# Sliding attention: where the score mask is added, and who copies the unrotated half of the queries

## The chip, the cores and the metric

One core of one Trainium2 chip runs the whole program. The metric is the device time of an execution in microseconds (us); of several executions the median counts.

## The reference, cut to what matters

The program applies eight layers to x (four batches of 512 tokens, 512 features): four attentions and four feed-forward blocks. The change lies in the last attention, which looks back over a window of 128 tokens, has 16 query heads of 128 features, one key and value head, and a sink logit per head:

```python
q = h @ wq_comp @ wq_up
q = q.reshape(b, t, H, D).transpose(0, 2, 1, 3)
q = _rmsnorm(_apply_partial_rope(q, cos, sin), q_norm_w)
k = _rmsnorm(_apply_partial_rope(h @ wk, cos, sin), k_norm_w)
v = h @ wv
mask = (diff >= 0) & (diff < WIN)
scores = jnp.einsum('bhtd,bsd->bhts', q, k) * scale
scores = jnp.where(mask[None, None], scores, jnp.asarray(-1e+30, h.dtype))
probs = jax.nn.softmax(jnp.concatenate([scores, sink], axis=-1), axis=-1)
attn = jnp.einsum('bhts,bsd->bhtd', probs[..., :t], v)
```

The partial rotation turns features 0 to 63 of each head; features 64 to 127 pass unchanged. `diff` is query index less key index.

## The kernel before, in words

Each layer is a function that opens blocks with one program per engine: TensorE (PE), VectorE (DVE), ScalarE (ACT), GpSimd (POOL) and the DMA queue of SyncE (SP). Engines wait for each other's semaphores. `window_attention` first merges the output weights in one block; the second block, in which the change lies, does the attention.

Its work comes in groups: 4 batches times 4 query tiles of 128 tokens times 4 groups of 4 heads, 64 groups G in all, 16 per batch (`PER`). The four groups of a batch's first query tile have one key tile (128 keys, narrow groups); the other twelve have the tile before as well (256 keys, wide groups). A list `ORDER` fixes the jobs of TensorE, and the other engines' programs are written by hand to match it:

- U: the projection of four heads of queries into bank 0, as three products (high and low parts). VectorE's `rotated` (through `rope`, lines 2317 to 2327) copies the unrotated half (L2322), does four multiplications (L2323 to L2326) and an addition (L2370), result in one of two SBUF tiles `q`.
- R: four transposes of `q` into bank 2 (L2505). ScalarE's `queries` copies them to `QT` (L2248). GpSimd squares `q` (L2195), VectorE sums the squares (L2374, `squares`), GpSimd takes the root, which gives the scale `qs`.
- S: the scores, two heads in bank 3 and two in bank 4. Per head one fp32 product of `QT` and `KT` (L2516, two instructions in the trace), and a bf16 product that adds the mask to the bank (L2518): the identity times `mask_b`, which holds 0 or −3e38 for the tile before and for the own tile.
- VectorE's `maxima`: per bank one reduction (L2380) gives the negated maxima of two heads; then `mt` (times the scale, L2388), `nm` (minimum with the negated sink, L2390), `si` (L2392).
- ScalarE's `exponentials`: four exponentials with their sums, straight from the banks (L2258), and the sink's (`es`, L2264). VectorE's `normalise`: `den` (L2398), a reciprocal, four scalings of the weights (L2403).
- PT: transposes of the weights into banks 5 and 6 (L2527), copied by ScalarE's `weights` to SBUF (L2271). O: weights times values into bank 7 (L2534). ScalarE copies the high part (L2278), VectorE subtracts for the low part (`low`, L2409). Y: twelve products of output and merged output weights (L101 to L103), added to x by VectorE after each query tile (L2414).

In iteration G TensorE does R of G+1, early jobs, U of G+2, Y of G−4, S of G+1, PT of G and O of G−1. The early jobs (`ahead`) are keys and values of this batch's later tiles (kv, kT) and the transposes (T, from VectorE's normalised rows `xn`, L2314), compression and first keys of the next batch. VectorE in iteration G: normalise G, low G−2, early jobs, rotate G+2, maxima G+1, squares G+2, and early in a batch the next batch's statistics and rows. ScalarE: exponentials G, queries G+1, outputs G−2, early jobs, weights G.

The same kind of fused operation that the change brings in stands in the first stage, at L759: a causal mask in SBUF is added to scores in a bank, in place, and the maximum goes to `mx`.

Of the kernel before, what the change touches and what calls it, by code (L numbers as in the profile page):

```python
# [16 lines left out]
F32 = mybir.dt.float32  # L17
# [3 lines left out]
ACT = mybir.ActivationFunctionType  # L21
# [3 lines left out]
P = 128  # L25
# [1952 lines left out]
def window_attention(prog, name, share):  # L1978
# [35 lines left out]
             ("ssq", "ms", "qs0", "qs", "mx", "mt", "nm", "si", "es", "rs", "den", "rec")}  # L2014
    ks = prog.sb(name + "_ks", [P, 2, 4], F32)


# [155 lines left out]

    with nc.Block() as block:
        @block.gpsimd
        def _(pool):
# [43 lines left out]
        def _(act):  # L2220
# [52 lines left out]
            def outputs(G):  # L2273
                act.wait_ge(*full("O", G))
                if G >= NG:
                    act.wait_ge(*projected(G - NG))
                n = G % NG
                act.activation(OT[0][:, HG * n:HG * n + HG, :], v4(ps[7][:, :]), ACT.Copy).then_inc(c["o_hi"].sem, 1)  # L2278

            for job in FIRST:  # L2280
                early(job)
            queries(0)
            for G in range(GROUPS):
                exponentials(G)
                if G + 1 < GROUPS:
                    queries(G + 1)
                if G >= 2:
                    outputs(G - 2)
                for job in ahead(G):
                    early(job)  # L2290
                weights(G)
# [4 lines left out]
        def _(dve):  # L2296
# [19 lines left out]

            def rope(dst, src, scratch, tt, heads, last_read):

                f = lambda ap: ap.rearrange("p (h n) -> p h n", h=heads)
                cos, sin, nsin = (trig[:, i, tt, :].unsqueeze(1).broadcast_to([P, heads, HALF]) for i in range(3))  # L2320
                d, s, t = f(dst), f(src), f(scratch)
                dve.tensor_copy(d[:, :, 2 * HALF:], s[:, :, 2 * HALF:])  # L2322
                dve.tensor_tensor(d[:, :, 0:HALF], s[:, :, 0:HALF], cos, ALU.mult)  # L2323
                dve.tensor_tensor(d[:, :, HALF:2 * HALF], s[:, :, HALF:2 * HALF], cos, ALU.mult)
                dve.tensor_tensor(t[:, :, 0:HALF], s[:, :, HALF:2 * HALF], nsin, ALU.mult)
                dve.tensor_tensor(t[:, :, HALF:2 * HALF], s[:, :, 0:HALF], sin, ALU.mult).then_inc(last_read, 1)  # L2326
                return d[:, :, 0:2 * HALF], t[:, :, 0:2 * HALF]
# [33 lines left out]
            def rotated(G):  # L2361
                dve.wait_ge(*full("U", G))
                if G >= 2:
                    dve.wait_ge(*full("R", G - 2))
                    dve.wait_ge(*c["q_sq"](0, G - 1))
                if G >= 1:
                    dve.wait_ge(*c["q_rot"](0, G))
                a, s = rope(q[G % 2][:, :], ps[0][:, :], wide_part, G % PER // NG, HG, J.frees(("U", G)))
                dve.wait_ge(*read("U", G))
                dve.tensor_tensor(a, a, s, ALU.add).then_inc(c["q_rot"].sem, 1)  # L2370
# [5 lines left out]
            def maxima(G):  # L2376
                i, lo = G % 2, (P if G % PER < NG else 0)
                for j in (0, 1):
                    dve.wait_ge(*full("S", G, j))
                    last = dve.tensor_reduce(small["mx"][:, i, 2 * j:2 * j + 2],  # L2380
                                             ps[3 + j][:, :].rearrange("p (h n) -> p h n", h=2)[:, :, lo:2 * P], AX.X, ALU.max,
                                             negate=True)
                last.then_inc(c["mx"].sem, 1)
# [3 lines left out]
                dve.wait_ge(*c["q_scale"](0, G + 1))  # L2387
                dve.tensor_tensor(small["mt"][:, i, :], small["mx"][:, i, :], small["qs"][:, i, :], ALU.mult).then_inc(c["mt"].sem, 1)  # L2388
                dve.wait_ge(*c["mt"](0, G + 1))
# [42 lines left out]
            rotated(1)  # L2432
            squares(1)
            maxima(0)
            for G in range(GROUPS):
# [27 lines left out]
        def _(pe):  # L2463
            for job in ORDER:
# [42 lines left out]
                elif kind == "S":  # L2507
# [4 lines left out]
                    for j in (0, 1):  # L2512
                        pe.wait_ge(*vacant("S", n, j))
                        for s in (0, 1):
                            hh = 2 * j + s
                            pe.matmul(ps[3 + j][:, s * 2 * P + lo:(s + 1) * 2 * P], QT[i][:, hh * P:(hh + 1) * P],  # L2516
                                      KT[:, k0:(tt + 1) * P], start=True, stop=False, skip_group_check=True)
                            last = pe.matmul(ps[3 + j][:, s * 2 * P + lo:(s + 1) * 2 * P], prog.ident_b[:, :],  # L2518
                                             prog.mask_b[:, :, :].rearrange("p m n -> p (m n)")[:, lo:2 * P], start=False,
                                             stop=True, skip_group_check=True)  # L2520
                        last.then_inc(J.fills(("S", n, j)), 1)
# [23 lines left out]
    J.close(1)  # L2545
    for count, n in ((c_stat, NB), (c_mv, NB), (c_var, NB), (c_rstd, NB), (c_xn, NT), (c_xhi, NT)):
        count.advance(n)
# [702 lines left out]
```

## Time and profile before

| | us |
|---|---|
| median of 3 runs | 3643.24 |
| lowest, highest | 3637.92, 3645.14 |
| the profiled execution's own time | 3647.04 |
| its span | 3645.1 |
| PE busy (share of the span) | 3166.7 (87%) |
| DVE busy | 1976.9 (54%) |
| ACT busy | 1255.9 (34%) |
| POOL busy | 704.7 (19%) |

The sliding attention's second block fills the span from about 2642 to 3250 us. Shares are averages over stages with different limits, so only the rows of that block bear on it. In a timeline each line is an instruction or a run of equal ones: start, duration, engine, line of the kernel, operation, output and inputs, count, and in brackets how long the engine stood idle before it and what released it. A product is recorded with its whole pipeline, so durations of neighbours overlap.

### The profile page before, as it was taken

How to read it: one execution, taken by the hardware profiler on the slowest of the kernel's cores; microseconds unless marked ns; L12 is line 12 of the kernel's file. 1: busy time of each engine (PE TensorE's matmuls, PEld its weight loads, DVE VectorE, ACT ScalarE, POOL GpSimd, SP SyncE). 2: the span in 40 equal slices, each digit the busy share in tenths (PEclk: the TensorE clock that was granted, in tenths of full speed). 3: DMA queues.
4: the chain of work that ended last, by engine and by line, in shares of the span. 5: the costliest groups of instructions: out<-in, count | busy, mean ns of one | idle time of the engine just before them, and what ended most of it. 6: DMA issues, size and time to landing. Idle time of an engine off the chain costs nothing. (4 is left out here: it accounts for less than half of the span.)

```text
span 3645.1 us, 51158 instructions
## 1 busy us (share of the span) xinstructions
PE 3166.7 (87%) x19428; PEld 2400.9 (66%) x19428; DVE 1976.9 (54%) x4840; ACT 1255.9 (34%) x2586; POOL 704.7 (19%) x875
## 2 busy tenths in 40 slices
PE   6999979998899996496888885899779999989999
PEld 4777767776667664344556664777357777768887
DVE  4445467776434434632365766766567777753221
ACT  2333245555223222013332225343534444441000
POOL 0111022222001000000014672000022332313222
PEclk8989989999798998687899987999889999999999
DMA  2000030002000003020310002000400000020000
GB/s 85 2 2 2 2 113 30 30 30 65 18 1 2 1 1 114 6 71 25 110 64 4 3 2 94 1 1 1 139 1 1 1 1 1 1 82 26 12 12 12
DMA packets 66184, 106.30 MB, mean 29 GB/s; under 512 B 9363, under 2 KB 29843, under 8 KB 65813
## 3 DMA queue, kind: packets, MB, share of 16 engines
q1 hardware_dynamic: 65526, 102.94, 8.2%
q8 instruction: 157, 2.57, 0.3%
q14 instruction: 85, 0.70, 0.1%
q0 software_dynamic: 416, 0.10, 0.0%
HBM read 90.27 MB, written 12.85 MB: 28 GB/s over the span
## 5 line engine op out<-in xcount | busy, mean ns | idle before, releaser
L401 ACT ACTIVATE tree_value<-tree_bit,table_lut,tree_step 128x256 f32<-128x256 uint8 x496 | 275.5, 595 | 136.5 <-DVE tree_value L415 65.3
L759 DVE CUSTOM_DVE_ANT_0 bank<-bank,a_causal 128x384 f32<-128x384 f32 (+3 forms) x512 | 235.8, 523 | 156.1 <-PE bank L868 156.1
L415 DVE COPY_PREDICATED tree_value<-tree_bit,tree_value 128x256 f32<-128x256 uint8 x434 | 237.1, 553 | 136.4 <-ACT tree_value L401 107.8
L101 PE MATMUL bank<-f_xT_hi,f_w_hi 128*128 128x512 f32 (+1 forms) x704 | 276.2, 392 | 8.1 <-DVE f_w_lo L1159 8.1
L102 PE MATMUL bank<-f_xT_hi,f_w_lo 128*128 128x512 f32 (+1 forms) x704 | 275.7, 392 | 0.0
L103 PE MATMUL bank<-f_xT_lo,f_w_hi 128*128 128x512 f32 (+1 forms) x704 | 275.6, 391 | 0.0
L684 ACT ACTIVATE a_PT<-bank 128x512 f32<-128x512 f32 (+1 forms) x384 | 174.4, 527 | 239.7 <-PE bank L881 239.5
L1083 POOL CAST f_h_hi<-f_sg 128x512 fp32r<-128x512 f32 (+1 forms) x88 | 84.0, 954 | 564.4 <-DVE f_sg L1180 293.6
L1182 DVE TENSOR_TENSOR f_sg<-bank,f_sg 128x512 f32<-128x512 f32 (+1 forms) x44 | 30.4, 691 | 270.6 <-PE bank L103 270.6
L101 PEld LDWEIGHTS bank<-f_xT_hi,f_w_hi 128*128 128x128 f32 (+1 forms) x704 | 132.5, 188 | 37.3 <-issue 8.8
L2271 ACT ACTIVATE a_PT<-bank 128x512 f32<-128x512 f32 x112 | 61.7, 595 | 276.7 <-PE bank L2527 276.7
L102 PEld LDWEIGHTS bank<-f_xT_hi,f_w_lo 128*128 128x128 f32 (+1 forms) x704 | 132.4, 188 | 28.9
L103 PEld LDWEIGHTS bank<-f_xT_lo,f_w_hi 128*128 128x128 f32 (+1 forms) x704 | 132.3, 188 | 29.0
L101 PE MATMUL bank<-f_w_hi,f_h_hi 128*128 128x512 f32 (+1 forms) x352 | 140.9, 400 | 6.0 <-POOL f_h_lo L1085 5.9
L2258 ACT ACTIVATE a_P<-bank,a_nm,a_qs 128x256 f32<-128x256 f32 (+1 forms) x256 | 134.4, 546 | 15.2 <-DVE a_nm L2390 14.9
L102 PE MATMUL bank<-f_w_hi,f_h_lo 128*128 128x512 f32 (+1 forms) x352 | 139.1, 395 | 0.0
L103 PE MATMUL bank<-f_w_lo,f_h_hi 128*128 128x512 f32 (+1 forms) x352 | 139.0, 395 | 0.0
L2516 PE MATMUL bank<-a_KT,a_QT 128*128 128x256 f32 (+1 forms) x512 | 131.8, 365 | 5.2 <-ACT a_QT L2248 5.1
L1117 ACT ACTIVATE f_sg<-bank 128x512 f32<-128x512 f32 (+1 forms) x44 | 26.3, 598 | 298.0 <-PE bank L103 298.0
L1085 POOL TENSOR_TENSOR f_h_lo<-f_sg,f_h_hi 128x512 fp32r<-128x512 f32 (+1 forms) x88 | 114.6, 1302 | 7.0
L1927 PE MATMUL bank<-f_fc,f_xT_hi 128*128 128x512 f32 x256 | 106.1, 415 | 6.3 <-issue 4.6
L2534 PE MATMUL bank<-a_PT,a_V 128*128 128x512 f32 x224 | 106.9, 594 | 1.4 <-DVE a_OT_lo L2409 1.4
(454 smaller groups left out, 8267.3 us busy)
## 6 DMA issues: line engine op xcount, KB each, us to landing
f_w_raw<-in_f_w SPq DMA_DIRECT2D x11, 768.0 KB, 12.8
f_w_raw<-table_w SPq DMA_DIRECT2D x11, 768.0 KB, 11.7
tree_idx<-in_f_idx SPq DMA_DIRECT2D x62, 128.0 KB, 2.2
table_w<-tree_value SPq DMA_DIRECT2D x62, 128.0 KB, 1.7
x_res<-in_x SPq DMA_DIRECT2D x4, 1024.0 KB, 9.5
m_piece<-in_m_wq SPq DMA_DIRECT2D x2, 2048.0 KB, 11.6
m_piece<-in_m_wo SPq DMA_DIRECT2D x2, 2048.0 KB, 8.8
m_piece<-in_m_w_gate SPq DMA_DIRECT2D x2, 2048.0 KB, 10.8
```

The costliest lines, as they stand in the source:

```text
L101: pe.matmul(out, w[0], x[0], start=first, stop=False, skip_group_check=True)
L102: pe.matmul(out, w[1], x[0], start=False, stop=False, skip_group_check=True)
L103: return pe.matmul(out, w[0], x[1], start=False, stop=last, skip_group_check=True)
L401: act.activation(prog.tree_value[(h + to) % 4][:, :], prog.tree_bit[h % 2][0][:, :], ACT.Identity, bias=prog.table_lut[:, 2 * k:2 * k + 1] ...
L415: dve.copy_predicated(prog.tree_value[(h + keep) % 4][:, :], prog.tree_bit[h % 2][bit][:, :], prog.tree_value[(h + other) % 4][:, :]).then ...
L684: act.activation(PT[j][:, g, :], ps[J.bank(key)][:, 0:WIDTH[j]], ACT.Exp, scale=scale).then_inc(J.frees(key), 1)
L759: last = dve.tensor_tensor_reduce(out=ps[J.bank(key)][:, col:col + n], in0=ps[J.bank(key)][:, col:col + n], in1=causal[:, T - n:T], scale= ...
L1085: pool.tensor_tensor(h[i % 2][1][0:n, :], sg[i % 2][0:n, :], h[i % 2][0][0:n, :].bitcast(F32), ALU.subtract).then_inc(c_lo.sem, 1)
L1927: last = pe.matmul(ps[n][:, :], xT[t % 2][i][:, k, :], fc[:, k, n * D:(n + 1) * D], start=k == 0 and i == 0, stop=k == DC - 1 and i == 1)
L2258: e = act.activation(Pr[i][:, hh, lo:2 * P], ps[3 + j][:, h2 * 2 * P + lo:(h2 + 1) * 2 * P], ACT.Exp, bias=small["nm"][:, i, hh:hh + 1], s ...
L2516: pe.matmul(ps[3 + j][:, s * 2 * P + lo:(s + 1) * 2 * P], QT[i][:, hh * P:(hh + 1) * P], KT[:, k0:(tt + 1) * P], start=True, stop=False, s ...
L2534: last = pe.matmul(ps[7][:, :], V[:, tt - 1 + j, :], PT[i][:, j, :], start=j == 0 or tt == 0, stop=j == 1)
```

## The change

TensorE no longer makes the mask product; a head's scores are one fp32 product. VectorE adds an fp32 mask, loaded into SBUF by one DMA at the block's head, to each head's scores in the bank, in place, and takes the maximum in the same operation: four such operations per group, each followed by a read of the accumulator, in place of two reductions. The maxima are no longer negated there; the operation for `mt` multiplies by −1. ScalarE copies the unrotated half of the queries (`passed`), after `outputs` and before the early jobs; VectorE waits for that count before it rotates.

```diff
+    mask = prog.sb(name + "_mask", [P, 2, P], F32)
+    c_mask, c_pass = prog.count("mask_in"), prog.count("q_pass")
...
+        @block.sync
+        def _(sp):
+            sp.dma_start(mask[:, :, :], ins["c_masks"].rearrange("m p n -> p m n")).then_inc(c_mask.sem, 16)
...
+            def passed(G):
+                act.wait_ge(*full("U", G))
+                if G >= 2:
+                    act.wait_ge(*full("R", G - 2))
+                    act.wait_ge(*c["q_sq"](0, G - 1))
+                act.activation(v4(q[G % 2][:, :])[:, :, 2 * HALF:], v4(ps[0][:, :])[:, :, 2 * HALF:], ACT.Copy).then_inc(c_pass.sem, 1)
+
             for job in FIRST:
                 early(job)
+            passed(0)
+            passed(1)
             queries(0)
...
                 if G >= 2:
                     outputs(G - 2)
+                if G + 2 < GROUPS:
+                    passed(G + 2)
                 for job in ahead(G):
                     early(job)
...
-                dve.tensor_copy(d[:, :, 2 * HALF:], s[:, :, 2 * HALF:])
+                if passed:
+                    dve.wait_ge(*c_pass(0, passed))
+                else:
+                    dve.tensor_copy(d[:, :, 2 * HALF:], s[:, :, 2 * HALF:])
...
-                for j in (0, 1):
-                    dve.wait_ge(*full("S", G, j))
-                    last = dve.tensor_reduce(small["mx"][:, i, 2 * j:2 * j + 2],
-                                             ps[3 + j][:, :].rearrange("p (h n) -> p h n", h=2)[:, :, lo:2 * P], AX.X, ALU.max,
-                                             negate=True)
+                window = mask[:, :, :].rearrange("p m n -> p (m n)")[:, lo:2 * P]
+                for hh in range(HG):
+                    j, at = hh // 2, hh % 2 * 2 * P
+                    if hh % 2 == 0:
+                        dve.wait_ge(*full("S", G, j))
+                    rows = ps[3 + j][:, at + lo:at + 2 * P]
+                    last = dve.tensor_tensor_reduce(out=rows, in0=rows, in1=window, scale=1.0, scalar=NEG, op0=ALU.add, op1=ALU.max,
+                                                    accum_out=small["mx"][:, i, hh:hh + 1])
...
-                dve.tensor_tensor(small["mt"][:, i, :], small["mx"][:, i, :], small["qs"][:, i, :], ALU.mult).then_inc(c["mt"].sem, 1)
+                dve.scalar_tensor_tensor(small["mt"][:, i, :], small["mx"][:, i, :], -1.0, small["qs"][:, i, :], ALU.mult,
+                                         ALU.mult).then_inc(c["mt"].sem, 1)
...
+            dve.wait_ge(*c_mask(0, 16))
             maxima(0)
...
-                            pe.matmul(ps[3 + j][:, s * 2 * P + lo:(s + 1) * 2 * P], QT[i][:, hh * P:(hh + 1) * P],
-                                      KT[:, k0:(tt + 1) * P], start=True, stop=False, skip_group_check=True)
-                            last = pe.matmul(ps[3 + j][:, s * 2 * P + lo:(s + 1) * 2 * P], prog.ident_b[:, :],
-                                             prog.mask_b[:, :, :].rearrange("p m n -> p (m n)")[:, lo:2 * P], start=False,
-                                             stop=True, skip_group_check=True)
+                            last = pe.matmul(ps[3 + j][:, s * 2 * P + lo:(s + 1) * 2 * P], QT[i][:, hh * P:(hh + 1) * P],
+                                             KT[:, k0:(tt + 1) * P], start=True, stop=True, skip_group_check=True)
```

The order of VectorE's instructions in one wide group near the end of batch 3, from the rotation to `si`, before:

```order
L2409 TENSOR_TENSOR a_OT_lo<-bank,a_OT_hi 128x512
L2322 COPY a_q_25906<-bank 128x4x64
L2323 TENSOR_TENSOR a_q_25906<-bank,a_trig 128x4x32
L2324 TENSOR_TENSOR a_q_25906<-bank,a_trig 128x4x32
L2325 TENSOR_TENSOR a_part<-bank,a_trig 128x4x32
L2326 TENSOR_TENSOR a_part<-bank,a_trig 128x4x32
L2370 TENSOR_TENSOR a_q_25906<-a_q_25906,a_part 128x4x64
L2380 TENSOR_REDUCE a_mx<-bank 128x2 x2
L2388 TENSOR_TENSOR a_mt<-a_mx,a_qs 128x4
```

and with the change, at the same place:

```order
L2433 TENSOR_TENSOR a_OT_lo<-bank,a_OT_hi 128x512
L2343 TENSOR_TENSOR a_q_25906<-bank,a_trig 128x4x32
L2344 TENSOR_TENSOR a_q_25906<-bank,a_trig 128x4x32
L2345 TENSOR_TENSOR a_part<-bank,a_trig 128x4x32
L2346 TENSOR_TENSOR a_part<-bank,a_trig 128x4x32
L2390 TENSOR_TENSOR a_q_25906<-a_q_25906,a_part 128x4x64
L2404 ISA bank,a_mx<-bank,a_mask 128x256
L2404 ISA a_mx 128x1
L2404 ISA bank,a_mx<-bank,a_mask 128x256
L2404 ISA a_mx 128x1
...
L2411 SCALAR_TENSOR_TENSOR a_mt<-a_mx,a_qs 128x4
```

The copy before the rotation is gone, and two reductions have become four pairs of a fused operation and an accumulator read (two pairs are left out).

ScalarE's order in the same place (`a_QT` is the query copy, `a_OT_hi` the output's high part, `a_PT` the transposed weights), before:

```order
L2264 ACTIVATE a_es<-a_si 128x4
L2248 ACTIVATE a_QT_25910<-bank 128x512
L2278 ACTIVATE a_OT_hi<-bank 128x512
L2271 ACTIVATE a_PT_25920<-bank 128x512 x2
L2258 ACTIVATE a_P_25917,a_rs<-bank,a_nm,a_qs 128x256 x4
```

and with the change:

```order
L2270 ACTIVATE a_es<-a_si 128x4
L2254 ACTIVATE a_QT_25910<-bank 128x512
L2284 ACTIVATE a_OT_hi<-bank 128x512
L2291 ACTIVATE a_q_25907<-bank 128x4x64
L2277 ACTIVATE a_PT_25920<-bank 128x512 x2
L2264 ACTIVATE a_P_25917,a_rs<-bank,a_nm,a_qs 128x256 x4
```

The copy of the unrotated half stands between the output's high part and the copies of the transposed weights.

## Rows read from the trace of the kernel before

**Rows 1.** windows, the stage: busy us (x) of PE, PEld, DVE, ACT, POOL, PEclk.
```profile
2670.00:3245.00 575.00, 555.90 (x2866) 421.77 (x2864) 427.61 (x1401) 277.60 (x859) 174.20 (x290) 0.98 0.00 1
```

**Rows 2.** groups by line, 2670 to 3250 us: the mask products.
```profile
L2518 PE MATMUL bank<-mask_b,ident_b 128*128 128x256 bf16 (+1 forms) x256 | 67.0, 262 | 0.0
```

**Rows 3.** timeline of PE, scores of a wide group: start us, us, engine.
```profile
3208.07 0.59 PE L2516 MATMUL bank<-a_KT,a_QT 128*128 128x256 f32 x2
3208.49 0.27 PE L2518 MATMUL bank<-mask_b,ident_b 128*128 128x256 bf16 x1
3208.60 0.60 PE L2516 MATMUL bank<-a_KT,a_QT 128*128 128x256 f32 x2
...
3210.23 1.04 PE L2527 MATMUL bank<-ident,a_P 128*128 128x128 f32 x8
```

**Rows 4.** timeline of PE, scores of a narrow group (128 keys).
```profile
3117.16 0.22 PE L2518 MATMUL bank<-mask_b,ident_b 128*128 128x128 bf16 x1
3117.22 0.44 PE L2516 MATMUL bank<-a_KT,a_QT 128*128 128x128 f32 x2
...
3117.88 0.61 PE L2527 MATMUL bank<-ident,a_P 128*128 128x128 f32 x4
...
3118.33 1.88 PE L2534 MATMUL bank<-a_PT,a_V 128*128 128x512 f32 x4
```

**Rows 5.** timeline of DVE, one plain wide group, from den to den.
```profile
3205.56 0.16 DVE L2398 TENSOR_TENSOR a_den<-a_rs,a_es 128x4 f32<-128x4 f32 x1 [1.95 <-ACT a_es L2264]
...
3207.63 0.41 DVE L2322 COPY a_q<-bank 128x256 f32<-128x256 f32 x1
3207.96 0.28 DVE L2323 TENSOR_TENSOR a_q<-bank,a_trig 128x128 f32<-128x128 f32 x1
...
3209.35 0.69 DVE L2380 TENSOR_REDUCE a_mx<-bank 128x2 f32<-128x512 f32 x1
...
3210.43 0.69 DVE L2380 TENSOR_REDUCE a_mx<-bank 128x2 f32<-128x512 f32 x1 [0.39 <-PE bank L2518]
...
3211.16 0.16 DVE L2388 TENSOR_TENSOR a_mt<-a_mx,a_qs 128x4 f32<-128x4 f32 x1
...
3214.26 0.16 DVE L2398 TENSOR_TENSOR a_den<-a_rs,a_es 128x4 f32<-128x4 f32 x1 [1.36 <-ACT a_es L2264]
```

**Rows 6.** timeline of DVE, a wide group that waits for no scores.
```profile
3146.11 0.16 DVE L2398 TENSOR_TENSOR a_den<-a_rs,a_es 128x4 f32<-128x4 f32 x1 [1.07 <-ACT a_es L2264]
...
3149.76 1.35 DVE L2380 TENSOR_REDUCE a_mx<-bank 128x2 f32<-128x512 f32 x2
3151.15 0.16 DVE L2388 TENSOR_TENSOR a_mt<-a_mx,a_qs 128x4 f32<-128x4 f32 x1
...
3154.26 0.16 DVE L2398 TENSOR_TENSOR a_den<-a_rs,a_es 128x4 f32<-128x4 f32 x1 [1.95 <-ACT a_es L2264]
```

**Rows 7.** timeline of DVE, first stage: the fused operation, 256 and 128 columns.
```profile
304.93 0.47 DVE L759 CUSTOM_DVE_ANT_0 bank<-bank,a_causal 128x256 f32<-128x256 f32 x1
305.31 0.14 DVE L759 DVE_READ_ACCUMULATOR2_ANT a_mx<- 128x1 f32 x1
...
108.83 0.33 DVE L759 CUSTOM_DVE_ANT_0 bank<-bank,a_causal 128x128 f32<-128x128 f32 x1
109.08 0.14 DVE L759 DVE_READ_ACCUMULATOR2_ANT a_mx<- 128x1 f32 x1
```

**Rows 8.** groups by shape, ACT, 2665 to 3250 us: the query copy.
```profile
L2248 ACT ACTIVATE a_QT<-bank 128x512 f32<-128x512 f32 x64 | 39.4, 615 | 3.9 <-PE bank L2505 3.9
```

**Rows 9.** DMA issues of the page: a transfer of the mask's size.
```profile
tree_idx<-in_f_idx SPq DMA_DIRECT2D x62, 128.0 KB, 2.2
```

**Rows 10.** timeline of PE: waits early in batches 0 and 1.
```profile
2678.90 0.49 PE L2516 MATMUL bank<-a_KT,a_QT 128*128 128x128 f32 x2 [4.01 <-ACT a_QT L2248]
...
2846.09 0.67 PE L2472 MATMUL bank<-ident,a_xn 128*128 128x128 f32 x4 [1.81 <-DVE a_xn L2314]
```

**Rows 11.** windows, 2845 to 2850 us, columns as in rows 1.
```profile
2845.00:2850.00 5.00, 3.91 (x13) 3.14 (x14) 4.15 (x13) 3.41 (x13) 1.55 (x3) 0.66 0.00 0
```

More of the change, by code:

```diff
@@ L2315, in scaled, with rope @@
                                   ALU.mult).then_inc(c_xn.sem, 1)
-            def rope(dst, src, scratch, tt, heads, last_read):
+            def rope(dst, src, scratch, tt, heads, last_read, passed=0):
                 f = lambda ap: ap.rearrange("p (h n) -> p h n", h=heads)
@@ L2367, in rotated @@
                     dve.wait_ge(*c["q_rot"](0, G))
-                a, s = rope(q[G % 2][:, :], ps[0][:, :], wide_part, G % PER // NG, HG, J.frees(("U", G)))
+                a, s = rope(q[G % 2][:, :], ps[0][:, :], wide_part, G % PER // NG, HG, J.frees(("U", G)), G + 1)
                 dve.wait_ge(*read("U", G))
@@ L2545, in window_attention @@
     J.close(1)
-    for count, n in ((c_stat, NB), (c_mv, NB), (c_var, NB), (c_rstd, NB), (c_xn, NT), (c_xhi, NT)):
+    for count, n in ((c_mask, 16), (c_pass, GROUPS), (c_stat, NB), (c_mv, NB), (c_var, NB), (c_rstd, NB), (c_xn, NT), (c_xhi, NT)):
         count.advance(n)
```

## The prediction, made before the run

> **What bounds the kernel now.** The change touches one stage, the sliding attention, so I first took the windows view of that stage [rows 1]: of 575 us TensorE shows 555.9 busy, VectorE 427.6, ScalarE 277.6. Busy time of a pipelined engine proves little, so the second view is the timeline of one group of four heads. In the group of rows 5 VectorE goes from one `den` to the next in 8.70 us and stands idle in it twice: 1.36 us until ScalarE's exponentials are done (1.95 us a group before), and 0.39 us until the second bank of scores is there. TensorE has no wait at all in these 8.70 us. Such a group is therefore bound by TensorE's issue, and what counts there is not the duration of a product but the distance from its start to the next start.
>
> The third view is the other loop. VectorE's maxima of a group release ScalarE's exponentials, these release `den`, and VectorE then works through weights, query rotation and the next maxima. In batch 3 stands a group in which the scores were ready before VectorE came, so that both maxima run back to back [rows 6]: den to den 3154.26 − 3146.11 = **8.15 us**. That is what the VectorE–ScalarE loop takes by itself; TensorE's 8.70 lies 0.55 above it. The whole forecast is a race of these two numbers.
>
> **The change part by part.** There are 64 groups (4 batches of 16), 48 wide (256 keys) and 16 narrow (128 keys), 256 heads in all.
>
> *Mask products go (TensorE).* The grouped row gives 256 of them, 67.0 us busy, 262 ns each [rows 2]. That is not the gain, since they overlap their neighbours. In a wide group the mask product starts at 3208.49 and the next head's scores at 3208.60: it holds the issue for 0.11 us [rows 3]. In a narrow group only 0.06 us lie between these two starts, but two heads take 3117.88 − 3117.22 = 0.66 us, 0.33 each for three products; four fp32 transposes of the same width take 3118.33 − 3117.88 = 0.45, also 0.11 each [rows 4]. So every product of that width is paced at 0.11, most likely by its weight load, and two products should take 0.22. I take 0.11 for each of the 256: **28.2 us**, 0.44 a group. The lower bound for the 64 narrow heads is the 0.06: 192 × 0.11 + 64 × 0.06 = 25.0 us. Nothing bounds it above but the 67.0, which would need the products not to overlap; rows 3 exclude that.
>
> The Trainium skill (TensorE: Matmul & The Clock Gate, Part 1, on the gap of 56 ns) has back-to-back starts at columns over 2.4 GHz plus some 2.5 ns: 109 ns for 256 columns, 56 ns for 128. The wide row agrees. For narrow heads the page would make the removal worth 56 ns, a sum of 24.5 us in place of 28.2, while the pace of rows 4 speaks for 0.11.
>
> *Maxima (VectorE).* Two reductions become four fused operations, each with an accumulator read. The same operation with the same operands (bank in and out, fp32 mask in SBUF) runs in the first stage: 256 columns step in 305.31 − 304.93 = 0.38 us, 128 columns in 109.08 − 108.83 = 0.25, and the closing read lasts 0.14 [rows 7]. Wide, to the start of `mt`: 4 × 0.38 + 0.14 + 0.05 = 1.71, against 3151.15 − 3149.76 = 1.39 now [rows 6]: +0.32. Narrow: 4 × 0.25 + 0.19 = 1.19. No narrow pair stands in the rows; half of the wide pair, 0.7, and the 1.39 bound it, so +0.5 to −0.2, and I take +0.4, near the first end, since a reduction's time goes with its columns. The negation moves into the `mt` operation, four elements either way, whose distance to the next operation is set by the start and not the elements: nothing.
>
> *Query copy (VectorE to ScalarE).* VectorE drops a copy that holds it for 3207.96 − 3207.63 = 0.33 us [rows 5]. So the VectorE–ScalarE loop changes by +0.32 − 0.33: it stays at about **8.14 us** wide, and +0.07 narrow. ScalarE's new copy has half the columns of the query copy of 615 ns [rows 8]; it costs between nothing and 0.62 us, I take 0.4, nearer the row since a fixed part stays. It stands behind two copies that follow the exponentials, and after it ScalarE waits for TensorE's transposed weights anyway, so it is hidden. What it now waits for is the projection U of group G+2; queued behind it are the T, kv and kT copies and the PT copies, and VectorE's rotation waits for it. The rotation comes after `den`, four scalings and the low half of the output, 3207.63 − 3205.56 = 2.07 us; three ScalarE copies of at most 0.62 end before that. If this cover goes (U late), the price is up to 0.4 us a group.
>
> *The mask transfer.* One DMA of 128 KB at the head of the block; one of that size landed in 2.2 us [rows 9], and it is needed only after projections, rotation and the first scores. SP's queue has nothing else in this block: nothing.
>
> *What becomes of 28.2 us.* In wide groups TensorE needs 8.70 − 0.44 = 8.26, still above 8.14, so the gain arrives in full there, with 0.12 us left. It also reaches the maxima: the second bank is full 0.44 earlier, and two fused operations take 2 × 0.38 + 0.19 = 0.95 from there, against 3211.16 − 3210.43 = 0.73 now: `mt` comes 0.2 earlier after the group's first scores, so VectorE keeps up. Kv and transposing groups add about as much to either engine.
>
> Where TensorE waits for VectorE, its own saving buys a longer wait. That is so early in the batches:
> - batches 1 and 2: TensorE waits 1.81 us for the next batch's normalised rows [rows 10], which VectorE makes behind its statistics; shorter waits follow in the next two tiles. Five groups of scores lie in that stretch (2.2 us saved), and VectorE's chain brings back only the 0.2 at each place where it waits for scores, less 0.07 in narrow groups: about 1.0 kept, 1.2 lost, twice: 2.4.
> - batch 0: the same, and the start, where TensorE waits 4.01 us for a query copy [rows 10]. Seven groups (3.1), 0.4 kept, and the start gets about 0.6 longer, because the rotations of groups 0 and 1 wait for ScalarE's copy (0.4 against 0.33, plus a handover each) and the first maxima are 0.4 longer: 3.3 lost.
> - batch 3: no next batch, but rows 6 show VectorE behind there; three groups, 1.2 lost.
> - the last group: its `mt` gains 0.2 of the 0.44: 0.2 lost.
>
> Sum: 28.2 − 2.4 − 3.3 − 1.2 − 0.2 = **21.1 us** off. The profiled execution took 3647.04 us (span 3645.1), so 3625.9; it is 3.8 above the median of the three runs, 3643.24, against which I forecast **3622.1 us**. Three runs spread over 7 us, so what can be told from no change is about 0.2%, 7 us.
>
> **The rivals.**
> - *The VectorE–ScalarE loop becomes the bound, slower than before.* Place: the four fused operations of a wide group. 8.14 against 8.26 leaves 0.03 us a head. At 0.38 + 0.03 the loop ties; the gain is gone where it reaches 8.70, 0.14 a head more (0.52). For it: each operation now reads a mask from SBUF and writes the bank back, beside GpSimd's squares; one reduction of 512 columns is split in two. Against: rows 7 are the same operation. If one took 0.55, the wide loop would be 8.14 + 4 × 0.17 = 8.82: the 20 groups that VectorE bounds already add 0.68 each (13.6), the other 37 wide ones 0.12 (4.4), so +18 us, 3661. The Trainium skill (Perfetto Trace Analysis, Optimizing Scalar/DVE Operations) puts about 125 ns of fixed time on a VectorE operation on PSUM and advises fewer, larger ones; by it two more operations alone are 0.25 us a group, which is within the +0.32 that the rows give.
> - *Hidden anyway.* If the slack that the profile shows on VectorE is not real (a wait I read as "for ScalarE" hides another), the saved issue turns into waits nearly everywhere and only 0.1 a group is kept: about 6 us, 3637 and above. For: 8.15 is close under 8.70. Against: the 0.39 us wait for scores in every plain group.
> - *All of it arrives*, the waits early in the batches shrinking with the rest: 28.2 off, 3615.
> - *More half-speed time.* Behind the 1.81 us wait the granted clock is 0.66 for five us [rows 11], a mixture of its two levels, where the stage has 0.98 [rows 1]. Longer waits could add such stretches: each of 5 us at 0.66 is worth some 1.7 us, three of them 5 us: 3627.
> - *ScalarE's place in line.* If U is late for its copy, everything queued behind is late; at 0.4 us in 20 groups 8 us of the gain, 3630.
>
> **How the numbers follow.** Forecast 0.72, with half-speed and partial loop loss inside its own range of 3613 to 3632; all of it 0.07; ScalarE's place 0.06; hidden 0.08; the loop 0.07. For 8 in 10 the range is 3612 to 3634: below, the full gain less 3 us of scatter between runs; above, ScalarE's case and scatter. Faster than 0.2% (below 3636) 0.86: the forecast, all of it, ScalarE's place and 0.01 of the hidden case; within 0.2% the other 0.07 of that and 0.01 of the loop's; slower 0.06, the rest of the loop's.
>
> **What would show it.** Right: no mask products; wide heads 0.43 us apart on TensorE; plain groups 8.26 us den to den; four fused operations stepping at 0.38; the 0.39 us wait for scores shrunk to near zero and that for exponentials still above 1 us; the 1.81 us wait grown to about 2.5; ScalarE's copies ended before the rotation. Wrong: fused operations at over 0.41 us a step; plain groups at 8.4 us or more with TensorE idle before the transposes of the weights or queries; VectorE idle before the rotation, released by ScalarE; narrow heads at 0.27 apart, not 0.22.

## The result, and the profile after

The changed kernel takes **3622.18 us** (median of 5 runs, 3612.82 to 3624.99), the kernel before 3644.19 us in the same series (5 runs, 3637.92 to 3648.39). The ratio is 0.9939, with a 95% interval of 0.9928 to 0.9951: 22 us less, where the prediction had 21.1 and 3622.1 us. That the two medians agree to 0.1 us is luck: the five runs of either kernel spread over 10 to 12 us.

| us | before | after |
|---|---|---|
| the profiled execution's own time | 3647.04 | 3612.82 |
| its span | 3645.1 | 3610.8 |
| the stage, from its first statistics to the next layer's | 617.86 | 595.16 |
| the rest of the span | 3027.2 | 3015.6 |
| PE, DVE, ACT busy in the span | 3166.7, 1976.9, 1255.9 | 3128.9, 1974.3, 1276.1 |

The two profiled executions lie 34 us apart, far more than the medians. The stage's limits in VectorE's timeline (start, duration, engine and line, operation, output and input, count) show why. Before:

```profile
2641.80 2.47 DVE L2299 BATCH_NORM_STATS2 stats<-x_res 128x6 f32<-128x512 f32 x4 [0.32 <-PEq L2023]
...
3259.66 2.47 DVE L1130 BATCH_NORM_STATS2 stats<-x_res 128x6 f32<-128x512 f32 x4 [0.32 <-PEq L2174]
```

The same limits after, and between them, for the readings below, rows of VectorE's timeline of this run: four `den` from the tiles in which the next batch is prepared, the maxima of a narrow group, and two wide groups:

```profile
2630.00 2.47 DVE L2316 BATCH_NORM_STATS2 stats<-x_res 128x6 f32<-128x512 f32 x4 [0.32 <-PEq L2025]
...
2831.03 0.16 DVE L2422 TENSOR_TENSOR a_den<-a_rs,a_es 128x4 f32<-128x4 f32 x1 [0.78 <-ACT a_es L2270]
...
2839.93 0.16 DVE L2422 TENSOR_TENSOR a_den<-a_rs,a_es 128x4 f32<-128x4 f32 x1 [0.61 <-ACT a_es L2270]
...
2969.77 0.16 DVE L2422 TENSOR_TENSOR a_den<-a_rs,a_es 128x4 f32<-128x4 f32 x1 [0.78 <-ACT a_es L2270]
...
2980.24 0.16 DVE L2422 TENSOR_TENSOR a_den<-a_rs,a_es 128x4 f32<-128x4 f32 x1 [0.61 <-ACT a_es L2270]
...
3096.87 0.29 DVE L2404 CUSTOM_DVE_ANT_0 bank<-bank,a_mask 128x128 f32<-128x128 f32 x1
...
3097.99 0.16 DVE L2411 SCALAR_TENSOR_TENSOR a_mt<-a_mx,a_qs 128x4 f32<-128x4 f32 x1
...
3124.27 0.16 DVE L2422 TENSOR_TENSOR a_den<-a_rs,a_es 128x4 f32<-128x4 f32 x1 [1.66 <-ACT a_es L2270]
...
3127.59 0.42 DVE L2404 CUSTOM_DVE_ANT_0 bank<-bank,a_mask 128x256 f32<-128x256 f32 x1
...
3129.25 0.16 DVE L2411 SCALAR_TENSOR_TENSOR a_mt<-a_mx,a_qs 128x4 f32<-128x4 f32 x1
...
3132.07 0.16 DVE L2422 TENSOR_TENSOR a_den<-a_rs,a_es 128x4 f32<-128x4 f32 x1 [1.67 <-ACT a_es L2270]
...
3181.10 0.16 DVE L2422 TENSOR_TENSOR a_den<-a_rs,a_es 128x4 f32<-128x4 f32 x1 [1.18 <-ACT a_es L2270]
...
3183.17 0.28 DVE L2343 TENSOR_TENSOR a_q<-bank,a_trig 128x128 f32<-128x128 f32 x1
...
3184.66 0.43 DVE L2404 CUSTOM_DVE_ANT_0 bank<-bank,a_mask 128x256 f32<-128x256 f32 x1 [0.15 <-PE bank L2541]
...
3185.01 0.47 DVE L2404 CUSTOM_DVE_ANT_0 bank<-bank,a_mask 128x256 f32<-128x256 f32 x1
3185.39 0.14 DVE L2404 DVE_READ_ACCUMULATOR2_ANT a_mx<- 128x1 f32 x1
...
3189.36 0.16 DVE L2422 TENSOR_TENSOR a_den<-a_rs,a_es 128x4 f32<-128x4 f32 x1 [1.78 <-ACT a_es L2270]
...
3225.16 2.47 DVE L1130 BATCH_NORM_STATS2 stats<-x_res 128x6 f32<-128x512 f32 x4 [0.32 <-PEq L2176]
```

The stage went from 3259.66 − 2641.80 = 617.86 to 3225.16 − 2630.00 = 595.16 us, **22.7 less**. The other 11.6 us lie outside it, in code that the change does not touch. In the nine profiled executions of this study that rest varies between 3015.6 and 3027.7 us, whatever was edited. It goes with the mean granted clock of the execution: the four at 0.916 (before, e2, e5, e6) have 3024.4 to 3027.7, the five at 0.919 or 0.920 have 3015.6 to 3020.4. The medians carry the same split (of 23 executions of the kernel before, 13 at a clock of 0.919 and above average 3637.3 us, ten at 0.918 and below 3646.1), so experiments are better compared by the stage.

**A plain wide group** (counterpart of [rows 5]) goes from `den` at 3181.10 to 3189.36: **8.26 us**, the 8.26 of the prediction. The 0.39 us wait for the second bank is gone, 0.15 us are left for the first, and `den` still waits 1.78 us for the exponentials: VectorE has slack, TensorE sets the pace. Against [rows 3, 4], the scores in TensorE's timeline after, narrow and then wide, and the three waits for the next batch's rows in batch 1 (one that bears on [rows 10]):

```profile
2830.30 0.66 PE L2497 MATMUL bank<-ident,a_xn 128*128 128x128 f32 x4 [1.89 <-DVE a_xn L2331]
...
2838.77 0.66 PE L2497 MATMUL bank<-ident,a_xn 128*128 128x128 f32 x4 [0.76 <-DVE a_xn L2331]
...
2847.25 0.66 PE L2497 MATMUL bank<-ident,a_xn 128*128 128x128 f32 x4 [0.43 <-DVE a_xn L2331]
...
3080.32 1.05 PE L2541 MATMUL bank<-a_KT,a_QT 128*128 128x128 f32 x8
3081.20 1.04 PE L2549 MATMUL bank<-ident,a_P 128*128 128x128 f32 x8
...
3183.60 1.89 PE L2541 MATMUL bank<-a_KT,a_QT 128*128 128x256 f32 x8
3185.32 1.04 PE L2549 MATMUL bank<-ident,a_P 128*128 128x128 f32 x8
```

Four wide heads take 3185.32 − 3183.60 = 1.72 us, 0.43 each, where a head took 0.54; four narrow ones 0.88, **0.22 each**, where it was 0.33. ScalarE's timeline of the same group, behind two rows near 3130 us that are read further down:

```profile
3128.19 1.08 ACT L2277 ACTIVATE a_PT<-bank 128x512 f32<-128x512 f32 x2 [2.70 <-PE bank L2549]
3129.65 0.56 ACT L2264 ACTIVATE a_P<-bank,a_nm,a_qs 128x256 f32<-128x256 f32 x1 [0.37 <-DVE a_nm L2414]
...
3181.89 0.43 ACT L2291 ACTIVATE a_q<-bank 128x256 f32<-128x256 f32 x1
3185.96 1.08 ACT L2277 ACTIVATE a_PT<-bank 128x512 f32<-128x512 f32 x2 [3.64 <-PE bank L2549]
```

The moved copy ends at 3182.3, 0.85 us before VectorE rotates at 3183.17, and ScalarE stands idle for 3.64 us right after it: hidden, as forecast. Over the stage, the groups by line and shape (2655 to 3215 us; busy us, mean ns of one, idle before):

```profile
L2404 DVE CUSTOM_DVE_ANT_0 bank<-bank,a_mask 128x256 f32<-128x256 f32 x192 | 77.7, 449 | 9.8 <-PE bank L2541 8.2
...
L2404 DVE DVE_READ_ACCUMULATOR2_ANT a_mx<- 128x1 f32 x256 | 36.0, 141 | 0.0
L2291 ACT ACTIVATE a_q<-bank 128x256 f32<-128x256 f32 x64 | 26.2, 410 | 15.4 <-PE bank L103 15.3
...
L2343 DVE TENSOR_TENSOR a_q<-bank,a_trig 128x128 f32<-128x128 f32 x64 | 18.1, 283 | 3.0 <-ACT a_q L2291 3.0
```

The mask products of [rows 2] have no row any more. ScalarE's copy costs 410 ns, and VectorE waited for it only 3.0 us in all, at two places at the start. ScalarE's 15.3 us of waiting for U are 64 short waits in time in which it otherwise stands idle for TensorE's transposes, as in the rows above.

### The profile page after: what moved, and what is told of

It reads as the page before. It is cut to its first block and busy times, and to the rows that moved or that the text cites. A ratio compares the mean times of both kernels' runs of the same rounds, so it can differ in the third digit from the quotient of the medians.

```text
span 3610.8 us, 51095 instructions
## 1 busy us (share of the span) xinstructions
PE 3128.9 (87%) x19172; PEld 2382.9 (66%) x19172; DVE 1974.3 (55%) x5160; ACT 1276.1 (35%) x2650; POOL 707.3 (20%) x875
## 5 line engine op out<-in xcount | busy, mean ns | idle before, releaser
L2541 PE MATMUL bank<-a_KT,a_QT 128*128 128x256 f32 (+1 forms) x512 | 109.3, 357 | 4.6 <-ACT a_QT L2254 4.6
```

## The experiments

The theory of the prediction is that TensorE's issue bounds the stage and gives all of the gain, with the VectorE–ScalarE loop just under it; the rivals give that loop, the moved copy, or slack that is not real the leading part. The runs stand in this table beside before and after (us). The parts are VectorE's from `den` to `den` of a batch's first group and the next batch's, b3 to the last group's `den`, behind which 20.0 us of the stage follow in every run; "plain" is the period of a plain wide group, "start" runs to the first `den`. Each ratio goes against the kernel before as it ran in the same series, whose median was 3644.19 us for the changed kernel, 3638.43 (23 runs) for e1 to e4 and 3644.14 (15 runs) for e5 to e7; medians of different series are not to be subtracted.

| | median | ratio to before, 95% | stage | start | b0 | b1 | b2 | b3 | plain |
|---|---|---|---|---|---|---|---|---|---|
| before | 3644.19 | | 617.86 | 36.59 | 142.43 | 146.44 | 146.43 | 125.96 | 8.70 |
| after | 3622.18 | 0.9939 [0.9928, 0.9951] | 595.16 | 37.39 | 138.35 | 138.75 | 140.32 | 120.35 | 8.25 |
| e1_copy_back | 3621.52 | 0.9944 [0.9931, 0.9958] | 598.35 | 36.85 | 137.91 | 139.33 | 142.00 | 122.24 | 8.13, 8.25 |
| e2_copy_only | 3636.81 | 0.9989 [0.9979, 0.9999] | 614.37 | 36.56 | 142.89 | 144.56 | 144.64 | 125.70 | 8.70 |
| e3_both_masks | 3644.27 | 1.0011 [0.9999, 1.0022] | 619.76 | 37.80 | 142.63 | 146.72 | 146.71 | 125.89 | 8.70 |
| e4_no_mask | 3621.84 | 0.9942 [0.9926, 0.9958] | 593.97 | 36.77 | 137.00 | 139.96 | 139.97 | 120.26 | 8.25 |
| e5_two_more | 3642.69 | 0.9999 [0.9987, 1.0010] | 615.82 | 38.71 | 142.89 | 145.30 | 144.40 | 124.52 | 8.45 |
| e6_rows_early | 3610.37 | 0.9914 [0.9897, 0.9930] | 584.55 | 36.48 | 134.33 | 136.69 | 136.70 | 120.34 | 8.25 |
| e7_rows_ahead | 3607.73 | 0.9911 [0.9894, 0.9927] | 582.51 | 37.13 | 133.25 | 136.09 | 135.71 | 120.32 | 8.25 |

**e3_both_masks: the VectorE part alone.** The changed kernel with the mask products put back; the mask in SBUF is cleared once, so the fused operations add zeros.

```diff
             dve.wait_ge(*c_mask(0, 16))
+            dve.memset(mask[:, :, :], 0.0).then_inc(c_mask.sem, 1)
+            dve.wait_ge(*c_mask(0, 17))
...
-                            last = pe.matmul(..., QT[i][...], KT[...], start=True, stop=True, ...)
+                            pe.matmul(..., QT[i][...], KT[...], start=True, stop=False, ...)
+                            last = pe.matmul(..., prog.ident_b[:, :], prog.mask_b[...], start=False, stop=True, ...)
```

> The changed kernel with TensorE's mask products put back; the fused operations add a mask of zeros (set once before the first group), so VectorE and ScalarE do exactly the work of the changed kernel. Theory A: plain wide groups at 8.70 us, the stage 616 to 621 us, the program 3642 to 3648, no gain left. Theory B: the gain stays, the stage near 597.

Measured: 3644.27 us, ratio 1.0011, no difference to be told; stage 619.76. Everything VectorE and ScalarE do is as in the changed kernel, and with TensorE's products back the stage is 24.6 us longer and the plain group is 8.70 again. So the fused operations and the moved copy give nothing by themselves (the stage is 1.9 us longer than before). In VectorE's timeline of this run:

```profile
3185.43 0.43 DVE L2404 CUSTOM_DVE_ANT_0 bank<-bank,a_mask 128x256 f32<-128x256 f32 x1 [0.38 <-PE bank L2545]
...
3186.51 0.43 DVE L2404 CUSTOM_DVE_ANT_0 bank<-bank,a_mask 128x256 f32<-128x256 f32 x1 [0.21 <-PE bank L2545]
```

VectorE waits for both banks of scores: the heads again come at TensorE's old pace.

**e4_no_mask: the TensorE part alone.** The kernel before without mask products and without anything in their place; the scores carry no mask at all.

```diff
-                            pe.matmul(..., QT[i][...], KT[...], start=True, stop=False, ...)
-                            last = pe.matmul(..., prog.ident_b[:, :], prog.mask_b[...], start=False, stop=True, ...)
+                            last = pe.matmul(..., QT[i][...], KT[...], start=True, stop=True, ...)
```

> The kernel before without its mask products and without a mask anywhere (every query sees all keys of its two tiles, nothing is hidden): VectorE keeps its two reductions and the copy. Theory A: TensorE's saving alone: plain wide groups at 8.25 us, the stage 594 to 600 us, the program 3621 to 3628. If the fused operations cost the changed kernel something, this one is faster than it by that; by the rows of the fused operation (+0.27 us) and of the copy (-0.33) in the groups that VectorE bounds I expect it equal within 3 us. Theory B: no gain.

Measured: 3621.84 us, stage 593.97, 23.9 less than before and only 1.2 less than the changed kernel. Of 28.2 us of issue that the products held, even a removal with no replacement gives back 23.9. The price of masking on VectorE, with the copy moved off it, can't be read from the 1.2 us between this stage and the changed kernel's: a stretch of half clock lies in batch 1 here and not there, and one costs the changed kernel as much in batch 0 and not here (about 1.5 us each, see below). Group by group it is small: from the eighth group of each batch on the two kernels' periods agree within 0.03 us.

**e2_copy_only: the moved copy alone,** in the kernel before.

```diff
+            passed(0)
+            passed(1)
             queries(0)
...
+                if G + 2 < GROUPS:
+                    passed(G + 2)
...
-                dve.tensor_copy(d[:, :, 2 * HALF:], s[:, :, 2 * HALF:])
+                if passed:
+                    dve.wait_ge(*c_pass(0, passed))
+                else:
+                    dve.tensor_copy(d[:, :, 2 * HALF:], s[:, :, 2 * HALF:])
```

> The kernel before with the moved copy alone: mask products and two reductions as before, ScalarE copies the unrotated half. Theory A: plain wide groups stay at 8.70 us, TensorE-bound; the groups that VectorE bounds gain up to 0.33: the stage 612 to 618 us (before 617.9), the program 3638 to 3644. Theory B: 21 us gained, the stage about 597, the program near 3623.

Measured: 3636.81 us (expected 3638 to 3644), ratio 0.9989, its interval just under 1; stage 3.5 shorter, in batches 1 and 2 (1.9 and 1.8), none in the plain groups, which stay at 8.70. The windows of this run right behind the 1.82 us waits for the next batch's rows (in the columns the clock is the third number from the end) show where it lies:

```profile
2844.00:2849.00 5.00, 5.00 (x26) 4.05 (x25) 3.89 (x14) 2.34 (x8) 1.51 (x3) 1.00 0.00 0
2988.00:2993.00 5.00, 4.63 (x23) 3.83 (x24) 4.11 (x15) 2.97 (x11) 1.55 (x3) 1.00 0.00 0
```

The granted clock is full there, and it was 0.66 in the kernel before [rows 11]. The group behind the wait takes 9.17 us in both batches where it took 10.72, 1.55 less; so most of this gain is the absent half-speed stretch, and the copy's 0.33 us shows once a batch, in the third narrow group (8.17 for 8.49). Where TensorE bounds, taking work from VectorE does nothing. Not even the three short groups of batch 3 gained what was expected: they take 7.84, 8.14 and 7.84 us, before 7.79, 8.15 and 7.82.

**e1_copy_back: the change without the moved copy.**

```diff
-            passed(0)
-            passed(1)
...
-                if G + 2 < GROUPS:
-                    passed(G + 2)
...
-                a, s = rope(q[G % 2][:, :], ps[0][:, :], wide_part, G % PER // NG, HG, J.frees(("U", G)), G + 1)
+                a, s = rope(q[G % 2][:, :], ps[0][:, :], wide_part, G % PER // NG, HG, J.frees(("U", G)))
```

> The change without the moved copy: mask by the fused operations, no mask products, but VectorE copies the unrotated half itself. Theory A (TensorE's issue bounds the plain groups, and the gain is the removed products): VectorE's loop grows from 7.80 to 8.13 us, still under TensorE's 8.25, so plain wide groups stay at 8.25 us and only some 20 groups that VectorE bounds add 0.33: the stage 595 + 6 = 599 to 603 us, the program 3626 to 3630. Theory B (the shorter VectorE loop brings the gain): the gain falls by 0.33 in all 64 groups, 21 us: the stage about 616, the program near 3643.

Measured: 3621.52 us, its ratio not to be told from the changed kernel's; stage 3.2 us longer at 598.35. Both lie under what was expected (3626 to 3630, 599 to 603), since far fewer than 20 groups had to pay the 0.33. Of the 3.2 us, 1.9 lie in batch 3, where TensorE waits 1.84 us for VectorE's addition to x (1.25 in the changed kernel) and has a granted clock of 0.66 in the five microseconds behind it. `den` in batch 3, from its timeline:

```profile
3173.01 0.16 DVE L2418 TENSOR_TENSOR a_den<-a_rs,a_es 128x4 f32<-128x4 f32 x1 [1.66 <-ACT a_es L2270]
...
3181.15 0.16 DVE L2418 TENSOR_TENSOR a_den<-a_rs,a_es 128x4 f32<-128x4 f32 x1 [1.66 <-ACT a_es L2270]
```

Here VectorE runs at its own pace, 3181.15 − 3173.01 = 8.14 us, which is still under TensorE's 8.25. It was 7.80 in the changed kernel (3132.07 − 3124.27 in the rows above), so the copy is worth 0.34 in the loop and next to nothing in the time.

**e5_two_more: the loop pushed over TensorE's pace.** The changed kernel with two more reductions of 256 columns per group, results unused.

```diff
                     dve.wait_ge(*c_pass(0, passed))
+                    for k in range(2):
+                        dve.tensor_reduce(extra[k][:, :], s[:, :, 2 * HALF:], AX.X, ALU.max)
```

> The changed kernel with two more small VectorE operations per group before the rotation (maxima of the unrotated half, 256 columns each, their results unused), some 0.35 us each. Theory A (TensorE bounds plain wide groups at 8.25 us, VectorE and ScalarE at 7.80): the loop becomes 8.50 and now sets the pace: plain wide groups 8.45 to 8.55 us, the stage 611 to 618 us (595.2), the program 16 to 23 us longer than the changed kernel. Rival (VectorE's slack is larger than the loop says, since e1 with 0.33 more cost only 3 us in the stage): plain groups stay at 8.25, the stage under 603.

Measured: ratio 0.9999, the whole gain gone; stage +20.7 against the changed kernel. From VectorE's timeline:

```profile
3187.44 0.17 DVE L2425 TENSOR_TENSOR a_den<-a_rs,a_es 128x4 f32<-128x4 f32 x1 [1.67 <-ACT a_es L2271]
...
3195.89 0.16 DVE L2425 TENSOR_TENSOR a_den<-a_rs,a_es 128x4 f32<-128x4 f32 x1 [1.67 <-ACT a_es L2271]
...
3197.96 0.74 DVE L2343 TENSOR_REDUCE a_extra<-bank 128x4 f32<-128x256 f32 x2
3198.62 0.28 DVE L2346 TENSOR_TENSOR a_q<-bank,a_trig 128x128 f32<-128x128 f32 x1
```

The two hold VectorE for 3198.62 − 3197.96 = 0.66 us; 7.80 + 0.66 = 8.46, and the plain group takes 3195.89 − 3187.44 = 8.45. This is the prediction's rival of the loop, made real: groups that VectorE already bounds pay 0.66, plain ones the 0.20 above 8.25. Against the changed kernel's periods, ten groups are 0.64 to 0.67 longer and 22 are 0.19 to 0.24 longer; the others lie between and around, as waits and the clock moved (the extremes are −1.08 and +2.22 us). So the prediction's count of 20 groups that VectorE bounds, which would give 13.2 + 44 × 0.20 = 22.0, comes near the 20.7 without being what happened. With e1 there are now three doses: a loop of 7.80, 8.14 and 8.46 us gives stages of 595.2, 598.4 and 615.8. The second step of 0.32 costs 17.4 where the first of 0.34 cost 3.2, far more than the 1.6 us of a half-speed stretch: the price breaks upward where the loop passes TensorE's pace.

**e6_rows_early and e7_rows_ahead: the wait that was left.** After the change TensorE's longest waits in batches 1 and 2 are for `xn`, the next batch's normalised rows. e6 makes statistics, GpSimd's roots and rows one group earlier:

```diff
-                if b + 1 < NB and g == 1:
+                if b + 1 < NB and g == 0:
                     statistics(b + 1)
-                if b + 1 < NB and 2 <= g <= 5:
-                    scaled(b + 1, g - 2)
+                if b + 1 < NB and 1 <= g <= 4:
+                    scaled(b + 1, g - 1)
```

> The changed kernel with the next batch's statistics in group 0 instead of 1 of a batch, its normalised rows in groups 1 to 4 instead of 2 to 5. If TensorE's waits for these rows (1.9, 0.8 and 0.4 us in a batch, some 11 us in the stage) are what the removed products could not bring in, the waits go, and TensorE meets the next bound, VectorE's loop in the narrow groups: the stage 588 to 593 us (595.2), the program 2 to 7 us faster than the changed kernel. If these waits only stand for VectorE's own chain, the wait moves to the query transposes and the stage stays within 1 us.

e7 takes the statistics out of the batch's first groups: those of batch 1 stand ahead of the first group, those of later batches, one tile at a time, in groups 8 to 11 two batches ahead; GpSimd's roots move with them.

```diff
+            statistics(1)
...
-                if b + 1 < NB and g == 1:
-                    statistics(b + 1)
+                if b + 2 < NB and 8 <= g < 8 + TT:
+                    statistics(b + 2, [g - 8])
-                if b + 1 < NB and 2 <= g <= 5:
-                    scaled(b + 1, g - 2)
+                if b + 1 < NB and 1 <= g <= 4:
+                    scaled(b + 1, g - 1)
```

> As the run before, and the statistics leave VectorE's loop: those of batch 1 are made at the stage's start, where VectorE waits 6.4 us for the compression, those of batches 2 and 3 one tile each in groups 8 to 11 of the batch before the last, while VectorE waits for ScalarE's exponentials. The 2.8 us of statistics then no longer hold up a narrow group: three times 1 to 2 us below the run before, the stage 583 to 589 us, the program 6 to 12 us faster than the changed kernel, 28 to 34 below the kernel before.

Measured: 3610.37 and 3607.73 us, ratios 0.9914 [0.9897, 0.9930] and 0.9911 [0.9894, 0.9927]. Both are faster than the kernel before; against the changed kernel's ratio of 0.9939 [0.9928, 0.9951] e7's interval lies clear below and e6's just touches it, and the stages are 10.6 and 12.7 us shorter. The two intervals do not tell e6 from e7. Both gains are larger than was expected (stages of 588 to 593 and 583 to 589 us). About 3 us of either come from two stretches of half clock that cost the changed kernel some 1.5 us each, in batches 0 and 2, and these kernels nothing; without them e6 would lie close to its range's low end and e7 inside its range. In TensorE's timeline of e6 all of the waits for `xn` inside the batches are gone; what is late next is the addition of the output to x:

```profile
2845.31 0.47 PE L101 MATMUL bank<-a_w_hi,a_OT_hi 128*128 128x512 f32 x1 [1.89 <-DVE x_res L2438]
...
2982.01 0.47 PE L101 MATMUL bank<-a_w_hi,a_OT_hi 128*128 128x512 f32 x1 [1.89 <-DVE x_res L2438]
```

In batch 1, where the clock was full in both kernels behind these waits, the changed kernel waited 0.74 + 1.89 + 0.76 + 0.43 = 3.8 us and e6 waits 1.89 plus 0.24 for queries, 1.7 less; the batch is 2.06 shorter (138.75 to 136.69). Where e6 has 1.89 us of wait for `x_res`, e7 has 1.36 and 1.41.

## Why the prediction was right, point by point

- **What bounds.** Shown: undoing TensorE's part alone (e3) costs the whole gain, making it alone (e4) brings it, and moving VectorE's copy (e2) brings nothing in any plain group. With it fall the rivals of hidden slack and of ScalarE's place in line: plain groups gave back the whole 0.44 us, and VectorE waited 3.0 us in all for ScalarE's copy.
- **28.2 us of issue.** Held: 0.54 to 0.43 us a wide head, 0.33 to 0.22 a narrow one. The Trainium skill (TensorE: Matmul & The Clock Gate, Part 1, on the gap of 56 ns) would have made the narrow removal worth 56 ns; the rows say 0.11 us, the pace read from the transposes. Its cause was a guess there ("most likely by its weight load"), and TensorE's weight loads of the kernel before bear it out for the narrow heads: scores, mask and scores again follow without a gap, three loads in 3117.50 − 3117.16 = 0.34 us.

```profile
3117.16 0.30 PEld L2516 LDWEIGHTS bank<-a_KT,a_QT 128*128 128x128 f32 x2
3117.38 0.10 PEld L2518 LDWEIGHTS bank<-mask_b,ident_b 128*128 128x128 bf16 x1
3117.50 0.30 PEld L2516 LDWEIGHTS bank<-a_KT,a_QT 128*128 128x128 f32 x2
```

- **Fused maxima.** Wide: 3129.25 − 3127.59 = 1.66 us to `mt` (predicted 1.71); narrow 3097.99 − 3096.87 = 1.12 (predicted 1.19). The step is the 0.38 of [rows 7]; the first one is shorter, 0.35. Against [rows 6] the wide ones cost +0.27 where +0.32 stood, but the pair of reductions there was held up by 0.07 (next point); the next group's pair, which was not, takes 3159.23 − 3157.91 = 1.32, so the price is **0.34**. Narrow it is the same: such a pair took 0.79 in the kernel before, and +0.4 had been taken. The Trainium skill (Perfetto Trace Analysis, Optimizing Scalar/DVE Operations) puts some 125 ns of fixed time on an operation on PSUM, an estimate of 0.25 for two more; the measured 0.34 lies somewhat over it, and holds the last accumulator read as well, 0.14 in the rows.
- **The VectorE–ScalarE loop: the mis-sized term.** I took 8.15 us as "what the loop takes by itself" and 8.14 after. It is **7.80**. From `den` to the first fused operation it is 3.32 where [rows 6] have 3.65 (the copy, −0.33), the maxima add 0.27, and `mt` to `den` fell from 3.11 to 2.82. In the group of [rows 6] the exponentials did not start on VectorE's signal: ScalarE was still copying the transposed weights. Nor were all its scores ready before VectorE came, as the prediction read: the last product into the second bank starts at 3150.12, 0.36 us after VectorE's first reduction. The timelines of before in that group, of ScalarE and TensorE, and VectorE's next pair of reductions:

```profile
3150.86 1.09 ACT L2271 ACTIVATE a_PT<-bank 128x512 f32<-128x512 f32 x2 [3.65 <-PE bank L2527]
3151.83 0.57 ACT L2258 ACTIVATE a_P<-bank,a_nm,a_qs 128x256 f32<-128x256 f32 x1
...
3150.12 0.27 PE L2518 MATMUL bank<-mask_b,ident_b 128*128 128x256 bf16 x1
...
3157.91 1.28 DVE L2380 TENSOR_REDUCE a_mx<-bank 128x2 f32<-128x512 f32 x2
3159.23 0.16 DVE L2388 TENSOR_TENSOR a_mt<-a_mx,a_qs 128x4 f32<-128x4 f32 x1
```

  The exponential has no wait of its own there and starts 0.68 us after `mt` (3151.15); in the changed kernel's rows it waits 0.37 us for `nm` and starts 0.40 after `mt` (3129.25). A part of the 8.15 was TensorE's pace, 0.29 us passed on through ScalarE and 0.07 through the scores. The trace of before had a hint of it, since the groups on either side of [rows 6] took 7.79 and 7.82 us. e4 shows the old loop by itself, as VectorE does the same work there as before and TensorE less:

```profile
3116.49 0.16 DVE L2398 TENSOR_TENSOR a_den<-a_rs,a_es 128x4 f32<-128x4 f32 x1 [1.07 <-ACT a_es L2264]
...
3124.27 0.16 DVE L2398 TENSOR_TENSOR a_den<-a_rs,a_es 128x4 f32<-128x4 f32 x1 [1.66 <-ACT a_es L2264]
```

  That is **7.78**, so fused operations and moved copy together add 0.02 (7.80), and without the moved copy 0.36 (8.14 in e1). The step of the prediction that the two about cancel held; the level did not. The margin under TensorE was therefore 0.45 us and not 0.12, and the rival of the loop was given more chance than it had: a fused operation could have cost 0.11 more per head before the tie. Had the margin been 0.12, e1's loop, 0.33 longer, could not have run under TensorE's pace.
- **The copy.** 0.41 us on ScalarE where I took 0.4, ended 0.85 before the rotation. Its use is small: without it (e1) the time cannot be told from the changed kernel's.
- **Losses early in the batches.** Predicted: 2.4 in batches 1 and 2 together, 3.3 for batch 0 and start, 1.2 in batch 3, 0.2 in the last group. By stage parts the gain was 4.1 in batch 0 (predicted 7.04 − 2.7 = 4.3), 7.7 and 6.1 in batches 1 and 2 (5.8 each), 5.6 in batch 3 up to the last `den` (15 × 0.44 − 1.2 = 5.4), and the start lost 0.8 (0.6). The sum, 22.7, is 1.6 over the 21.1, and batch 1 alone is 1.9 over. That batch 0 came out as forecast is luck: one of its groups takes 10.13 us in the changed kernel where the same group of batches 1 and 2 takes 8.58 and 8.59, with a granted clock of 0.67 in 2698 to 2703 us. Without these 1.5 us the gain there would be 5.6 (e4 has 5.4), so the 2.7 us that were written off in batch 0 were some 1.3 too many.
- **Why batch 1 gained more.** The group behind the wait took 2839.93 − 2831.03 = 8.90 us in batch 1, and 2980.24 − 2969.77 = 10.47 in batch 2, after the same 1.89 us wait. The difference, 1.57, is clock. The changed kernel's windows there:

```profile
2830.00:2835.00 5.00, 4.70 (x23) 3.97 (x24) 4.11 (x15) 2.91 (x11) 1.54 (x3) 1.00 0.00 0
...
2970.00:2975.00 5.00, 5.00 (x17) 3.94 (x17) 3.79 (x13) 1.76 (x5) 1.06 (x3) 0.72 0.00 0
```

  In the kernel before both batches had the stretch, so here one was lost, and no run shows why. The rival "more half-speed time" had its price about right (1.7 us a stretch, 1.57 here), but the sum over the stage hardly moved: one stretch less in batch 1, and one more that costs time in batch 0.
- **A wait that did not grow as forecast.** I said the 1.81 us wait would grow to about 2.5. It grew to 1.89; the wait for the rotated queries ahead of it grew from 0.30 to 0.74, and those of the second and third tile from 0.59 and 0.26 to 0.76 and 0.43. The saved issue came back as waits, as forecast, but spread over four places: 0.44 + 0.08 + 0.17 + 0.17 = 0.86 us a batch, where I took 1.2. It closes the sum: 7.04 − 0.86 = 6.2 against 6.1 measured in batch 2, and with 1.57 of clock 7.75 against 7.7 in batch 1.

## What to carry to other kernels

Work moved from one engine to another is worth what it held the bounding engine's issue for (here 0.11 us a product, not its 262 ns), and costs nothing on the other engine as long as that engine's own loop stays under the pace. That loop must be read from a group in which nothing in it waits on the bounding engine, not even by way of a third one; then the price of each further operation is small up to the crossing (3.2 us in 64 groups for 0.34 each in e1) and what exceeds the pace beyond it. What remains after such a change is the waits in the places where the other engine was already late, and moving that work (the next batch's rows) earlier took about half as much again off the stage as the change did (10.6 and 12.7 us after 22.7, about 3 of them the clock's).

## What the runs showed that I had not expected

- The half-speed stretch behind a wait is not decided by the wait's length. After waits of 1.81 to 1.89 us for `xn` the five microseconds that follow had a granted clock of 0.66 in both batches 1 and 2 of before, e3 and e4, of 1.00 and 0.66 in the changed kernel, of 1.00 and 0.50 in e1, of 0.50 and 0.66 in e5 (waits of 1.89 and 1.88), and of 1.00 in both in e2. What decides it stays open; at about 1.6 us each, two such stretches are as large as the effects that e1 and e2 were made to measure.
- The rest of the program, untouched, takes 3015.6 to 3027.7 us from execution to execution. A single profiled pair can be 12 us off by that alone, half of this change's gain; with the mean granted clock beside each, most of the difference can be told (0.916 and 0.919 for the pair of this case).
